# Attention and routed experts on one core: sink sums, denominators and small routing operations on GpSimd, the steps of a group in another order, the last residual added by VectorE

## The chip, the core and the metric

One core of a Trainium2 chip. The time is that of one execution on the device, in microseconds, the median of several. Engines: TensorE (PE in the profile), VectorE (DVE), ScalarE (ACT), GpSimd (POOL), and SyncE (SP), which issues most DMAs. Each engine works through its own instructions in order; between engines there are only semaphores.

## The reference

```python
x = x + attn(layernorm(x), W_qkv, W_out, s)      # x: 4 x 512 x 256
x = x + moe(layernorm(x), gating_w, w1, b1, w2, b2)

# attn: 32 query heads, 8 key/value heads, head size 64
q, k, v = split(x @ W_qkv);  q, k = rope(q), rope(k)
a = where(band mask, -inf, q k^T / 8)             # 512 x 512 for each head
w = softmax(concat([a, sink]))[..., :-1]          # one sink logit for each head
out = (w v) @ W_out

# moe: 8 experts, top 2, capacity 640 rows for each expert
gates = softmax(x @ gating_w);  weights, experts = top_k(gates, 2), normalised
position of each (token, choice) within its expert = running count
rows of each expert: relu(rows w1 + b1) w2 + b2, weighted and added to the token
```

All is float32.

## The kernel before, in words

The attention of a batch is worked off by key/value head: a group `g` is one batch and one key/value head with its four query heads, 32 groups in all, and each has 16 units `n` (head and row tile of 128 queries by 512 keys). `all_periods` (L300) walks the engines through 33 periods of 16 steps. At step `n` of period `g` it calls the engine's step function three times: `step(n, g)`, `step(n - 16, g + 1)` (preparing the next group) and `step(n + 16, g - 1)` (finishing the last one). The tables `PROJ_AT`, `ROT_AT`, `PV_AT` and so on (L283 to L294) say at which `n` of a group a piece is done, from -16 to 31. Since all engines walk through the same order, these tables are the order of each engine's queue.

PE (L1106): at every even step two score matmuls (a pair, L1120), each into one of three banks, so a pair waits for the row maximum of the first unit of the pair before. After them, by the tables: one of three projections of the next group (KV at -16, Q01 at -12, Q23 at -6, L1094), the turning of v (-8, L1101), the products of the last group with v in four pieces of 5, 3, 5 and 3 blocks (18, 20, 22, 24, L1139), and the output projection y in two halves (28, 30, L1152).

DVE (L853): for every unit the mask, scaling, row maximum and copy to SBUF in one instruction (L858), two units behind it a 32 by 32 transpose of two units of probabilities (L869). At 16 the sink logit plus row maximum for 16 units (`sink_arg`, L876), at 17 the denominator (`denom`, L886), its reciprocal and the turning of it. SP sends that through DRAM to `recip_wide` (L411, L419); at 26 and 27 DVE multiplies the four banks of P·V by it (`heads_sb`, L902).

ACT (L684): the exponential with its row sum for every unit (L691), copies of the projected chunk from PSUM one step after each projection (L673), of v (L681), the sink exponential at 16 (L703), and copies of y at 29 and 31 (L699).

POOL (L575): rotates each projected chunk (L568 to L571) once SP has copied the swapped halves of it (L374: two DMAs for KV, four for Q01 and Q23); KV at -13, Q01 at -8, Q23 at -2. After KV it splits the weights of a later group in high and low part (L539, L541). It adds y to the residual (L588) at 29 and 31. The first pair of a group waits for Q01's rotation and a second copy of k (`k_twice`), pair 8 for Q23's.

SP, for each group: swap of KV, reciprocals out and spread, swap of Q01, `k_twice`, load of weights, v out and in, for three groups the load of the next batch's normalised x, swap of Q23, and for the first eight groups zeroes for the slot rows.

Routing of batch b runs in the 96 steps that begin two periods after its last group's first step (`dve_route`, L924, and the like for other engines): statistics, root and transposes in the first 32, normalisation, logits in 32 to 47, top two, gates, weights, counting and slots in 48 to 63, and eight indirect DMAs on POOL, from 64 on, that scatter rows to expert slots (L605). Nearly all small sums were DVE's. For the last batch the same steps run alone, after all groups. Then the eight experts follow.

Of the kernel before, what the change touches and what calls it, by code (L numbers as in the profile page):

```python
# [59 lines left out]
def moe_layer(nc, x, w_qkv, w_out, sink, gate_w, w1, b1, w2, b2, rope, out):  # L60
    ctx = ExitStack()
    with ctx:
# [112 lines left out]
        s_centred = sem("s_centred")  # L175
        s_shifted = sem("s_shifted")
        s_gate_exp = sem("s_gate_exp")
# [152 lines left out]

# [19 lines left out]
        def _(sp):  # L350
# [113 lines left out]
            for g in range(GROUPS - 1):  # L464
# [52 lines left out]
        def _(pool):  # L517
# [57 lines left out]
            def pool_step(n, g, j):  # L575
# [6 lines left out]
                if n in RESIDUAL_AT:  # L582
# [7 lines left out]

            def pool_route(r, b, last):
                if r == IDS_AT:
                    if b > 0:
                        pool.wait_ge(s_scattered, b * (16 * TPB * TOPK))
                    nc.gpsimd.iota(xn2[:, :, D:D + 1].bitcast(U32), pattern=[[P, TPB], [0, 1]], base=b * L,
                                   channel_multiplier=1).then_inc(s_ids, 1)
                if r in SCATTER_AT:
                    c = SCATTER_AT[r]
                    if c == 0:
                        pool.wait_ge(s_routed, b + 1)  # L600
                        pool.wait_ge(s_zero_rows, 16 * E)
                        pool.wait_ge(s_ids, b + 1)
                    if c % TOPK == 0:
                        pool.wait_ge(s_norm2, b * TPB + c // TOPK + 1)
# [49 lines left out]
        def _(act):  # L654
# [29 lines left out]
            def act_step(n, g, j):  # L684
# [9 lines left out]
                if n in RESIDUAL_AT:  # L694
# [6 lines left out]
                if n == SINK_AT:  # L701
                    act.wait_ge(s_sink_arg, g + 1)
                    nc.scalar.activation(sink_exp[:, :], sink_arg[:, :], ACT.Exp).then_inc(s_sink_exp, 1)  # L703
# [26 lines left out]
            def act_route(r, b, last):  # L730
# [12 lines left out]
                if r == INDEX_AT:  # L743
# [64 lines left out]
        def _(dve):  # L808
# [44 lines left out]
            def dve_step(n, g, j):  # L853
# [20 lines left out]
                if n == SINK_AT:  # L874
                    dve.wait_ge(s_neg_max, g * UNITS + UNITS)
                    nc.vector.tensor_tensor(  # L876
                        sink_arg[:, :].rearrange("p (c t h) -> p c t h", c=PAIRS, h=2),
                        neg_max[j][:, :].rearrange("p (c t h) -> p c t h", c=PAIRS, h=2),
                        sink_all[:, (g % NKV) * QM:(g % NKV + 1) * QM].rearrange("p (c h) -> p c h", h=2).unsqueeze(2)
                        .broadcast_to([P, PAIRS, TPB, 2]), ALU.add).then_inc(s_sink_arg, 1)  # L880
                if n == RECIP_AT:
                    dve.wait_ge(s_probs, g * UNITS + UNITS)
                    dve.wait_ge(s_sink_exp, g + 1)
                    if later(g):
                        dve.wait_ge(s_recip_out, g * 16)
                    nc.vector.tensor_tensor(denom[:, :], sums[j][:, :], sink_exp[:, :], ALU.add).then_inc(s_denom, 1)  # L886
                    dve.wait_ge(s_denom, 2 * g + 1)

                    nc.vector.reciprocal(recip[:, 0:UNITS].rearrange("p (c h t) -> p c t h", c=PAIRS, h=2),
                                         denom[:, :].rearrange("p (c t h) -> p c t h", c=PAIRS, h=2)  # L890
                                         ).then_inc(s_denom, 1)
                    dve.wait_ge(s_denom, 2 * g + 2)
                    nc.vector.transpose(recip_t[:, :], recip[:, :]).then_inc(s_recip, 1)
                if n in HEADS_AT:
# [11 lines left out]
                    ins.then_inc(s_heads, 1)  # L906
            nc.vector.memset(recip[:, :], 0.0)
# [16 lines left out]
            def dve_route(r, b, last):  # L924
# [19 lines left out]
                if r == MEAN_PART_AT:  # L944
                    step(nc.vector.tensor_tensor(mean_part[:, :, :],
                                                 mean_var[:, 0:TPB, 0].unsqueeze(2).broadcast_to([P, TPB, E]),
                                                 gate_cols[:, :].unsqueeze(1).broadcast_to([P, TPB, E]), ALU.mult))

                if r == CENTRE_AT:
                    dve.wait_ge(s_logits, b + 1)  # L950
                    nc.vector.tensor_tensor(logits[:, :, :], PV[2][:, 0:TPB * E].rearrange("p (t e) -> p t e", e=E),
                                            mean_part[:, :, :], ALU.subtract).then_inc(s_centred, 1)
                if r == SCALE_AT:
                    dve.wait_ge(s_centred, b + 1)
                    step(nc.vector.tensor_tensor(logits[:, :, :], logits[:, :, :],
                                                 rstd[:, 0:TPB].unsqueeze(2).broadcast_to([P, TPB, E]), ALU.mult))
                if r == TOP_AT:
                    for t in range(TPB):
                        nc.vector.max(top_val[:, t, :], logits[:, t, :]).then_inc(s_top, 1)
                if r == SHIFT_AT:  # L960
                    dve.wait_ge(s_top, b * (2 * TPB) + TPB)
                    nc.vector.tensor_tensor(gates[:, :, :], logits[:, :, :],
# [356 lines left out]
```

## Time and profile before

| | |
|---|---|
| median of 3 runs | 1205.47 us (1203.82 to 1209.72) |
| profiled execution | 1205.47 us, its span 1203.7 us |
| PE busy | 1084.9 us, 90% |
| DVE busy | 936.7 us, 78% |
| POOL busy | 711.7 us, 59% |
| ACT busy | 642.7 us, 53% |

The groups of attention take the span up to about 920 us, the routing of the last batch and the way to the first expert up to 952 us, the experts the rest. A row of the timeline has the start, the duration, the engine, the line of the kernel, the operation, what it writes and reads, and how many instructions were merged in it; in brackets stand the idle time of the engine just before and who ended it.

### The profile page before, as it was taken

To read this page: it belongs to the slowest core of one execution; us is meant where nothing else is said; L and a number is where in the kernel's file an instruction comes from. 1 tells how busy PE (TensorE), PEld (TensorE's weight loads), DVE (VectorE), ACT (ScalarE), POOL (GpSimd) and SP (SyncE) were. 2 spreads that over 40 slices of the span, in tenths; PEclk is the share of its full clock that TensorE was granted. 3 is DMA by queue.
4 is the path that set the end of the run, shared out by engine and by line. 5 is a ranking of instruction groups with operands and counts; after the bars stand their busy time and mean duration, and the time that the engine had idled before them with its cause. 6 is when DMAs were issued, how large, how long until landed. Compare 5 with 4: busy or idle time off the path is not lost. (4 is left out here: it accounts for less than half of the span.)

```text
span 1203.7 us, 30733 instructions
## 1 busy us (share of the span) xinstructions
PE 1084.9 (90%) x12411; PEld 724.5 (60%) x12411; DVE 936.7 (78%) x2001; ACT 642.7 (53%) x1517; POOL 711.7 (59%) x534
## 2 busy tenths in 40 slices
PE   3589999999999999999899999989986499999996
PEld 1345555555555555555555555555545499999995
DVE  6789999889998989999898999888894144444442
ACT  1455665556755655575556657555553244555551
POOL 5566666666556776666586666567621555555552
PEclk9699999999999999999999999999997599999998
DMA  8343533333332422334333223223232414444441
GB/s 208 133 112 108 154 102 95 110 105 84 96 110 69 110 75 73 87 94 117 79 108 91 69 73 98 77 74 92 78 113 72 152 19 110 111 111 111 109 110 19
DMA packets 116286, 117.94 MB, mean 98 GB/s; under 512 B 35184, under 2 KB 103856, under 8 KB 115248
## 3 DMA queue, kind: packets, MB, share of 16 engines
q1 hardware_dynamic: 108848, 107.43, 30.9%
q0 software_dynamic: 7296, 8.55, 4.3%
q8 instruction: 98, 1.61, 0.6%
q14 instruction: 44, 0.36, 0.1%
HBM read 77.31 MB, written 24.97 MB: 85 GB/s over the span
## 5 line engine op out<-in xcount | busy, mean ns | idle before, releaser
L691 ACT ACTIVATE probs_ring<-probs_ring,neg_max 128x512 f32<-128x512 f32 x512 | 367.0, 717 | 349.0 <-DVE neg_max L858 348.7
L858 DVE CUSTOM_DVE_ANT_0 probs_ring<-bank,mask,sink_neg 128x512 f32<-128x512 f32 x512 | 365.4, 738 | 78.1 <-PE bank L1120 76.7
L869 DVE STREAM_TRANSPOSE probs_t<-probs_ring 128x1024 f32<-128x1024 f32 x256 | 317.0, 1238 | 0.0
L1120 PE MATMUL bank<-qk_st 64*128 64x512 f32 x1024 | 291.4, 646 | 17.0 <-DVE neg_max L858 15.5
L1139 PE MATMUL bank<-probs_t,v_quads 32*64 32x256 f32 x8192 | 258.3, 385 | 30.3 <-DVE probs_t L869 29.9
L1139 PEld LDWEIGHTS bank<-probs_t,v_quads 32*64 32x64 f32 x8192 | 175.5, 133 | 121.0 <-DVE probs_t L869 56.9
L568 POOL TENSOR_TENSOR chunk_sb<-chunk_sb,rope_sb 128x512 f32<-128x512 f32 (+1 forms) x96 | 123.2, 1283 | 158.6 <-DMA swap_sb<-chunk_sb 92.6
L588 POOL TENSOR_TENSOR x_sb<-x_sb,y_sb 128x512 f32<-128x512 f32 x64 | 81.6, 1275 | 179.2 <-ACT y_sb L699 179.1
L1120 PEld LDWEIGHTS bank<-qk_st 64*128 64x128 f32 x1024 | 77.4, 185 | 111.8 <-issue 66.2
L1094 PE MATMUL bank<-xcur,w_hi 128*128 128x512 f32 x384 | 132.6, 427 | 5.4 <-ACT v_next L681 3.5
L1152 PE MATMUL bank<-wo_sb,heads_sb 128*128 128x256 f32 x512 | 127.3, 392 | 0.9 <-DVE heads_sb L902 0.9
L1152 PEld LDWEIGHTS bank<-wo_sb,heads_sb 128*128 128x128 f32 x512 | 92.1, 189 | 58.3 <-issue 46.2
L571 POOL TENSOR_TENSOR qk_st<-chunk_sb,swap_sb 128x512 f32<-128x512 f32 (+1 forms) x96 | 122.5, 1276 | 7.5
L569 POOL TENSOR_TENSOR swap_sb<-swap_sb,rope_sb 128x512 f32<-128x512 f32 (+1 forms) x96 | 123.3, 1285 | 0.0
L1094 PEld LDWEIGHTS bank<-xcur,w_hi 128*128 128x128 f32 x384 | 66.0, 192 | 88.1 <-issue 49.1
L691 ACT ACTIVATION_READ_ACCUMULATOR probs_ring<-probs_ring,neg_max 128x1 f32 x512 | 95.4, 186 | 0.0
L1269 PE MATMUL bank<-w_hi,hidden_hi 128*128 128x256 f32 x320 | 91.0, 284 | 0.0
L784 ACT ACTIVATE hidden<-bank,b_sb 128x320 f32<-128x320 f32 x128 | 60.6, 525 | 56.4 <-PE bank L1256 56.4
L1269 PE MATMUL bank<-w_hi,hidden_lo 128*128 128x256 f32 x320 | 90.3, 282 | 0.0
L1269 PE MATMUL bank<-w_lo,hidden_hi 128*128 128x256 f32 x320 | 90.3, 282 | 0.0
L640 POOL TENSOR_TENSOR w_lo<-w_raw,w_hi 128x2048 fp32r<-128x2048 f32 x8 | 36.8, 4596 | 88.0 <-ACT w_hi L762 76.9
L1256 PE MATMUL bank<-slots_hi,w_hi 128*128 128x320 f32 x256 | 80.3, 314 | 1.4 <-issue 1.4
(127 smaller groups left out, 1493.3 us busy)
## 6 DMA issues: line engine op xcount, KB each, us to landing
v_quads<-v_rows SPq DMA_DIRECT2D x128, 128.0 KB, 2.6
recip_wide<-recip_rows SPq DMA_DIRECT2D x64, 256.0 KB, 4.4
w_raw<-in_L_ffn_w SPq DMA_DIRECT2D x16, 1024.0 KB, 6.6
swap_sb<-chunk_sb SPq DMA_DIRECT2D x320, 32.0 KB, 2.2
w_raw<-in_L_attn_W_qkv SPq DMA_DIRECT2D x32, 256.0 KB, 2.9
slot_rows<-x2T SPq DMA_DIRECT2D x8, 662.5 KB, 5.0
slots<-slot_rows SPq DMA_DIRECT2D x8, 662.5 KB, 4.0
w_raw<-in_L_attn_W_qkv SPq DMA_DIRECT2D x64, 64.0 KB, 2.7
```

The lines of the kernel that those rows point to most:

```text
L568: nc.gpsimd.tensor_tensor(straight, straight, rope_sb[rows, 0, :], ALU.mult).then_inc(s_pool, 1)
L569: nc.gpsimd.tensor_tensor(swapped, swapped, rope_sb[rows, 1, :], ALU.mult).then_inc(s_pool, 1)
L571: nc.gpsimd.tensor_tensor(qk_st[j][rows, PAIRS if c == KV else c - Q01, :], straight, swapped, ALU.add).then_inc(s_rot, 1)
L588: nc.gpsimd.tensor_tensor(x_sb[:, t:t + 2, :], x_sb[:, t:t + 2, :], y_sb[half][:, :, :], ALU.add).then_inc(s_residual, 1)
L691: nc.scalar.activation(probs[n % RING][:, :], probs[n % RING][:, :], ACT.Exp, bias=neg_max[j][:, n:n + 1], scale=-1.0, accum_out=sums[j][: ...
L858: nc.vector.tensor_tensor_reduce(probs[n % RING][:, :], SCORE[SCORE_OF[n // 2][n % 2]][:, :], mask[:, L - P - t * P:2 * L - P - t * P], -S ...
L869: nc.vector.transpose(probs_t[j][:, :, (h // 2) * (2 * P):(h // 2 + 1) * (2 * P)] .rearrange("p b (h q) -> p h b q", h=2)[:, :, :, t * BLK ...
L1094: ins = nc.tensor.matmul(PROJ[:, :], w[:, kc, chunk_cols(c)], xcur[g // NKV % 2][:, part, kc, :], start=(kc == 0 and m == 0), stop=(kc == ...
L1120: nc.tensor.matmul(SCORE[SCORE_OF[n // 2][hh]][:, :], qk_st[j][half, h // 2, t * P:(t + 1) * P], qk_st[j][half, PAIRS, :], start=True, sto ...
L1139: ins = nc.tensor.matmul(PV[a][p * HD:(p + 1) * HD, 0:2 * P], v_quads[j][rows, d, c * HD:(c + 1) * HD], probs_t[j][rows, blk, p * 2 * P:(p ...
L1152: ins = nc.tensor.matmul(PV[half][:, (a % 2) * D:(a % 2 + 1) * D], heads_sb[:, a, h * P:(h + 1) * P], wo_sb[:, bass.ds((g % NKV) * 2 + h, ...
L1269: ins = nc.tensor.matmul(FFN2[s][:, 0:D], a[:, c, s * P:(s + 1) * P], w[:, c, :], start=(c == 0 and m == 0), stop=(c == HC - 1 and m == 2))
```

## The change

The tables become (the others stay):

```diff
-        PROJ_AT = {-16: KV, -12: Q01, -6: Q23}
-        TURN_V_AT, V_NEXT_AT = -8, -7
-        ROT_AT = {-13: KV, -8: Q01, -2: Q23}
-        for n, blocks in [(18, 5), (20, 3), (22, 5), (24, 3)]:
-        SINK_AT, RECIP_AT = 16, 17
-        HEADS_AT = {26: 0, 27: 1}
-        Y_AT = {28: 0, 30: 1}
-        RESIDUAL_AT = {29: 0, 31: 1}
+        PROJ_AT = {-16: KV, -8: Q01, -2: Q23}
+        TURN_V_AT, V_NEXT_AT = -4, -3
+        ROT_AT = {-12: KV, -5: Q01, 2: Q23}
+        for n, blocks in [(18, 5), (20, 5), (22, 6)]:
+        SINK_AT, DENOM_AT, RECIP_AT = 16, 17, 19
+        HEADS_AT = {24: 0, 25: 1}
+        Y_AT = {26: 0, 28: 1}
+        RESIDUAL_AT = {27: 0, 29: 1}
...
-        TURN_X_AT = 16 + 12
-        X2T_AT = {16 + 13: 0, 16 + 14: 1}
+        TURN_X_AT = 16 + 14
+        X2T_AT = {16 + 15: 0, 32: 1}
-        IDS_AT = 32 + 9
-        LOGITS_AT = {32 + 12: 0, 32 + 14: 1}
-        MEAN_PART_AT, CENTRE_AT, SCALE_AT = 32 + 13, 32 + 15, 48
-        TOP_AT, SHIFT_AT, INDEX_AT, ONEHOT_AT, CHOSEN_AT = 49, 50, 51, 52, 53
-        GATE_SUM_AT, GATES_AT, TOP_SUM_AT, WEIGHTS_AT = 54, 55, 56, 58
-        COUNT_AT = 48 + 12
-        PLACE_AT, PICK_AT, SLOT_AT = 48 + 13, 48 + 14, 48 + 15
-        SCATTER_AT = {64: 0, 64 + 10: 1, 64 + 12: 2, 64 + 14: 3, 80: 4, 80 + 10: 5, 80 + 12: 6, 80 + 14: 7}
+        IDS_AT, MEAN_PART_AT = 32 + 9, 32 + 10
+        LOGITS_AT, CENTRE_AT, SCALE_AT = 32 + 14, 32 + 15, 48
+        TOP_AT, SHIFT_AT, INDEX_AT, GATE_EXP_AT, ONEHOT_AT, CHOSEN_AT = 50, 51, 51, 52, 53, 54
+        GATE_SUM_AT, GATES_AT, TOP_SUM_AT, WEIGHTS_AT = 54, 56, 57, 59
+        COUNT_AT = 48 + 14
+        PLACE_AT, PICK_AT, SLOT_AT, INDICES_AT = 48 + 15, 64, 66, 67
+        SCATTER_AT = {72: 0, 73: 1, 74: 2, 78: 3, 79: 4, 88: 5, 89: 6, 90: 7}
```

In SP's queue the swap of Q01 moves behind `k_twice` and the load of weights:

```diff
-                swap_halves(g + 1, Q01)
                 k_twice(g + 1, (g + 1) % 2)
                 if g + 3 < GROUPS:
                     load_w(g + 3, (g + 3) % 2)
+                swap_halves(g + 1, Q01)
```

The sink sum and the denominator leave DVE for POOL, with the same operands; DVE keeps the reciprocal and its turning, which wait for `s_denom`, and ACT's sink exponential waits for the denominator of the group before:

```diff
+                if n == SINK_AT:
+                    pool.wait_ge(s_neg_max, g * UNITS + UNITS)
+                    nc.gpsimd.tensor_tensor(
...
+                        .broadcast_to([P, PAIRS, TPB, 2]), ALU.add).then_inc(s_sink_arg, 1)
+                if n == DENOM_AT:
+                    pool.wait_ge(s_probs, g * UNITS + UNITS)
+                    pool.wait_ge(s_sink_exp, g + 1)
+                    if later(g):
+                        pool.wait_ge(s_recip, g)
+                    nc.gpsimd.tensor_tensor(denom[:, :], sums[j][:, :], sink_exp[:, :], ALU.add).then_inc(s_denom, 1)
```

In the routing of batches 0 to 2 eight products and sums of 32 or 64 elements and the update of `slot_base` go to POOL; for the last batch they stay on DVE. One of them stands for all:

```diff
+                if r == GATES_AT and not last:
+                    pool.wait_ge(s_gate_inv, b + 1)
+                    scale_gates(nc.gpsimd).then_inc(s_gates, 1)
+                    pool.wait_ge(s_gates, b + 1)
+                    pool.wait_ge(s_chosen, b + 1)
+                    gates_of_chosen(nc.gpsimd).then_inc(s_top_gates, 1)
```

The others are `mean_part_of`, `scale_logits`, `shift_logits`, `mark_chosen`, `weights_of`, `pick`, each at its step of the table. The two halves of the logits become one stretch of matmuls.

In the last group ACT's copies of y and POOL's residual adds are replaced by

```diff
+                if n in RESIDUAL_AT and g == GROUPS - 1:
+                    half = RESIDUAL_AT[n]
+                    t = (B - 1) * TPB + 2 * half
+                    dve.wait_ge(s_y, 2 * g + half + 1 + 1)
+                    dve.wait_ge(s_residual, 2 * g + half)
+                    nc.vector.tensor_tensor(x_sb[:, t:t + 2, :], x_sb[:, t:t + 2, :],
+                                            PV[half][:, :].rearrange("p (t d) -> p t d", t=2),
+                                            ALU.add).then_inc(s_residual, 1)
```

## Rows read from the trace of the kernel before

**Rows 1.** Page, busy time: us, share of the span, instructions.

```profile
PE 1084.9 (90%) x12411; PEld 724.5 (60%) x12411; DVE 936.7 (78%) x2001; ACT 642.7 (53%) x1517; POOL 711.7 (59%) x534
```

**Rows 2.** Timeline of ACT, sink exponentials: start us, us, engine, line, operation.

```profile
283.73 0.22 ACT L703 ACTIVATE sink_exp<-sink_arg 128x16 f32<-128x16 f32 x1
...
370.89 0.20 ACT L703 ACTIVATE sink_exp<-sink_arg 128x16 f32<-128x16 f32 x1
...
475.36 0.22 ACT L703 ACTIVATE sink_exp<-sink_arg 128x16 f32<-128x16 f32 x1
...
501.54 0.22 ACT L703 ACTIVATE sink_exp<-sink_arg 128x16 f32<-128x16 f32 x1
...
586.50 0.20 ACT L703 ACTIVATE sink_exp<-sink_arg 128x16 f32<-128x16 f32 x1
...
717.00 0.22 ACT L703 ACTIVATE sink_exp<-sink_arg 128x16 f32<-128x16 f32 x1 [0.15 <-DVE sink_arg L876]
...
802.48 0.20 ACT L703 ACTIVATE sink_exp<-sink_arg 128x16 f32<-128x16 f32 x1
```

**Rows 3.** Timeline of one plain period, 457 to 478 us; idle time before in brackets.

```profile
457.52 1.13 PE L1120 MATMUL bank<-qk_st 64*128 64x512 f32 x4
...
460.93 1.13 PE L1120 MATMUL bank<-qk_st 64*128 64x512 f32 x4
...
463.71 1.13 PE L1120 MATMUL bank<-qk_st 64*128 64x512 f32 x4
...
464.87 0.75 DVE L858 CUSTOM_DVE_ANT_0 probs_ring<-bank,mask,sink_neg 128x512 f32<-128x512 f32 x1 [0.19 <-PE bank L1120]
...
466.36 1.13 PE L1120 MATMUL bank<-qk_st 64*128 64x512 f32 x4
...
467.00 0.72 ACT L691 ACTIVATE probs_ring<-probs_ring,neg_max 128x512 f32<-128x512 f32 x1 [0.52 <-DVE neg_max L858]
...
467.72 0.57 ACT L673 ACTIVATE chunk_sb<-bank 128x512 f32<-128x512 f32 x1
...
469.48 1.13 PE L1120 MATMUL bank<-qk_st 64*128 64x512 f32 x4
...
472.46 1.13 PE L1120 MATMUL bank<-qk_st 64*128 64x512 f32 x4
...
475.92 1.23 DVE L869 STREAM_TRANSPOSE probs_t<-probs_ring 128x1024 f32<-128x1024 f32 x1
...
477.21 2.42 PE L1139 MATMUL bank<-probs_t,v_quads 32*64 32x256 f32 x80 [0.97 <-DVE probs_t L869]
```

**Rows 4.** Tile sink_arg (min/median/max ns), then POOL groups (busy us, mean ns).

```profile
L876 DVE TENSOR_TENSOR sink_arg<-neg_max,sink_all x32: 131/1031/1198, 73.8 to 904.9; 128x16 f32<-128x16 f32 x32
...
L595 POOL IOTA xn<- 128x4 uint32 x4 | 0.6, 140 | 0.0
```

**Rows 5.** Timeline and landings of the Q01 swap; last, a Q23 swap's landings.

```profile
457.46 2.46 SPq L374 DMA_DIRECT2D swap_sb<-chunk_sb  x4
...
462.79 1.28 POOL L568 TENSOR_TENSOR chunk_sb<-chunk_sb,rope_sb 128x512 f32<-128x512 f32 x1 [2.38 <-DMA swap_sb<-chunk_sb]
...
465.39 1.29 POOL L571 TENSOR_TENSOR qk_st<-chunk_sb,swap_sb 128x512 f32<-128x512 f32 x1
...
DMA to landing us min/median/max: 2.5/3.0/3.3
...
DMA to landing us min/median/max: 2.0/2.0/2.2
```

**Rows 6.** Timeline, first period's pairs and the last residual add.

```profile
60.36 1.13 PE L1120 MATMUL bank<-qk_st 64*128 64x512 f32 x4 [1.27 <-DVE neg_max L858]
...
71.59 1.13 PE L1120 MATMUL bank<-qk_st 64*128 64x512 f32 x4 [1.44 <-DVE neg_max L858]
...
921.58 1.26 POOL L588 TENSOR_TENSOR x_sb<-x_sb,y_sb 128x512 f32<-128x512 f32 x1 [0.77 <-ACT y_sb L699]
```

More of the change, by code:

```diff
@@ new lines, in shift_logits, with mark_chosen, scale_gates @@
+        def shift_logits(eng):
+            return eng.tensor_tensor(gates[:, :, :], logits[:, :, :],
+                                     top_val[:, :, 0].unsqueeze(2).broadcast_to([P, TPB, E]), ALU.subtract)
+        def mark_chosen(eng):
+            return eng.tensor_tensor(chosen[:, :, :], onehot[:, :, 0, :].bitcast(F32),
+                                     onehot[:, :, 1, :].bitcast(F32), ALU.add)
+        def scale_gates(eng):
+            return eng.tensor_tensor(gates[:, :, :], gates[:, :, :],
+                                     gate_sum[:, :].unsqueeze(2).broadcast_to([P, TPB, E]), ALU.mult)
@@ L580, in pool_step @@
                         split(g + 1, 1 - j, (g + 1) // 2)
-                if n in RESIDUAL_AT:
+                if n in RESIDUAL_AT and g < GROUPS - 1:
                     half = RESIDUAL_AT[n]
@@ L596, in pool_route @@
                                    channel_multiplier=1).then_inc(s_ids, 1)
+                if r == MEAN_PART_AT and not last:
+                    pool.wait_ge(s_rstd, b + 1)
+                    mean_part_of(nc.gpsimd).then_inc(s_mean_part, 1)
+                if r == SCALE_AT and not last:
+                    pool.wait_ge(s_centred, b + 1)
+                    scale_logits(nc.gpsimd).then_inc(s_scaled, 1)
+                if r == SHIFT_AT and not last:
+                    pool.wait_ge(s_top, b * (2 * TPB) + TPB)
+                    shift_logits(nc.gpsimd).then_inc(s_shifted, 1)
+                if r == CHOSEN_AT and not last:
+                    pool.wait_ge(s_onehot, b + 1)
+                    mark_chosen(nc.gpsimd).then_inc(s_chosen, 1)
+                if r == GATES_AT and not last:
[4 more added lines that the diff above has]
+                    gates_of_chosen(nc.gpsimd).then_inc(s_top_gates, 1)
+                if r == WEIGHTS_AT and not last:
+                    pool.wait_ge(s_top_inv, b + 1)
+                    weights_of(nc.gpsimd).then_inc(s_weights, 1)
+                if r == PICK_AT and not last:
+                    pool.wait_ge(s_place, b + 1)
+                    pick(nc.gpsimd).then_inc(s_picked, 1)
+                    nc.gpsimd.tensor_tensor(slot_base[:, :], slot_base[:, :], batch_total[:, :],
+                                            ALU.add).then_inc(s_slot_base, 1)
                 if r in SCATTER_AT:
@@ L702, in act_step @@
                     act.wait_ge(s_sink_arg, g + 1)
+                    if later(g):
+                        act.wait_ge(s_denom, g)
                     nc.scalar.activation(sink_exp[:, :], sink_arg[:, :], ACT.Exp).then_inc(s_sink_exp, 1)
@@ L961, in dve_route @@
                     dve.wait_ge(s_top, b * (2 * TPB) + TPB)
-                    nc.vector.tensor_tensor(gates[:, :, :], logits[:, :, :],
-                                            top_val[:, :, 0].unsqueeze(2).broadcast_to([P, TPB, E]),
-                                            ALU.subtract).then_inc(s_shifted, 1)
+                    if last:
+                        shift_logits(nc.vector).then_inc(s_shifted, 1)
                 if r == INDEX_AT:
@@ L976, in dve_route @@
                                             ALU.mult, ALU.add)
-                    dve.wait_ge(s_onehot, b + 1)
-                    step(nc.vector.tensor_tensor(chosen[:, :, :], onehot[:, :, 0, :].bitcast(F32),
-                                                 onehot[:, :, 1, :].bitcast(F32), ALU.add))
+                    if last:
+                        dve.wait_ge(s_onehot, b + 1)
+                        mark_chosen(nc.vector).then_inc(s_chosen, 1)
                 if r == GATE_SUM_AT:
@@ L1020, in dve_route @@
                                                    ALU.mult, ALU.add).then_inc(s_routed, 1)
-                    if not last:
-                        step(nc.vector.tensor_tensor(slot_base[:, :], slot_base[:, :], batch_total[:, :], ALU.add))
             dve.wait_ge(s_gate_cols, 1)
```

118 lines of the change are left out of this document (70 added, 48 removed).

## The prediction

> **What bounds the kernel now.** The page first: over the span PE is busy 90%, DVE 78%, POOL 59% [rows 1]. A share of 90% says that PE nearly bounds, not what its idle time waits for. So I read one period (16 steps, 8 pairs of score matmuls) from the timeline. The sink exponentials of ACT, one in each period, give its length: 501.54 − 475.36 = 26.18 us in a plain period, and 87.16, 84.96 and 85.48 us for the three periods together in which the steps of routing of a batch lie (370.89 − 283.73, 586.50 − 501.54, 802.48 − 717.00) against 78.5 for three plain ones [rows 2]. Routing costs 8.6 + 6.4 + 6.9 = 22 us.
>
> In the plain period the start times of the score pairs [rows 3] give the length of each PE slot, a pair (1.06 us to the next matmul) with what follows it: pair 10 to 12 (a projection) 466.36 − 463.71 = 2.65; 6 to 8 (five blocks of P·V) 460.93 − 457.52 = 3.41; 14 to 0 (half of y) 2.98; 12 to 14 (the other half) 3.12, of which about 0.14 is a wait for a row maximum; 8 to 10 (turning v, three blocks) 2.78. A K/V projection is as long as the others. The one large wait is at the first P·V block: 0.97 us for a DVE transpose [rows 3]. Followed back, DVE works without a pause from 464.87 (it had waited 0.19 for pair 10) to the end of that transpose at 475.92 + 1.23 = 477.15, and in that stretch lies the sink sum, 1.03 us in the median [rows 3, 4]. So the loop that sets the period is PE from P·V to pair 10, then DVE to the transpose: neither engine alone. PE without any wait would need about 25 us.
>
> **The change, part by part.**
>
> *Sink sum and denominator to POOL.* The sink sum takes 131 ns at the least and 1031 in the median on DVE [rows 4]; 0.95 of the period's DVE chain goes. The denominator stands behind the transpose, off that chain; its removal and the three steps by which the reciprocal comes later only give DVE slack. On POOL no add of 16 elements is in the trace. From below I take the iota of 4 elements, 140 ns [rows 4]; from above an add of 512 elements, 1.26 [rows 4, 6]. I take 0.2, by the iota. POOL then holds, from the period's start, two residual adds (2.5), sink sum (to 2.7), denominator after ACT's exponential (to 3.3); the swapped Q23 chunk lands at about 4.5, so even 1.26 each is hidden in a plain period. Queued behind a late denominator are the rotations of Q23 and K/V; Q23 is wanted at 13.4.
>
> Why the DVE form takes up to 1.2 us: its minimum is 0.13 and the rest is about one POOL add long, as if it waited for POOL. The Trainium skill (SBUF — State Buffer, Who interferes with whom) says that a DVE instruction with two SBUF inputs and a GpSimd one that reads SBUF exclude each other for the whole instruction; by that rule the trace agrees (131 against 1031 ns). The skill (Perfetto Trace Analysis, Optimizing Scalar/DVE Operations) warns that moving work between those two might therefore not help; by it the removal would still take the 0.9 of waiting off DVE, and POOL could at worst wait for a short DVE add.
>
> *The order of a group.* New PE slots, from the same rows: 0: K/V projection 2.65; 2: P·V of five 3.41; 4: five 3.41; 6: six 3.41 + 0.47 = 3.88; 8: Q01 projection 2.65; 10: y 2.98; 12: turning v (2.78 − 1.06 − 1.48 for three blocks = 0.24) and y 3.22; 14: Q23 2.65. The transpose for the first P·V ends at 1.16 + 2 × 0.67 + 1.24 + 0.06 = 3.8 after pair 0, PE is there at 3.71: wait 0.1. Pair 0 to pair 8 is 13.45. DVE has 16 reductions of at most 0.75, 8 transposes of 1.23, four head products (two take about 0.7 of the 2.13 below) and under 1 for the reciprocal: 12.0 + 9.8 + 1.4 + 1.0 = 24.2 at most, less than PE's 25, and is no bound.
>
> But Q01 is projected at pair 8 in place of 4, and its rotation must be done before pair 0 of the next group. That chain, from pair 8: to the DVE reduction 1.16 (463.71 to 464.87); reduction, two head products, reduction, to ACT's exponential 2.13 (to 467.00); to the chunk copy 0.72 (467.72), its 0.57 and 0.03 to the first of four swap DMAs; the last of these is issued 1.88 later and lands after 2.0 to 2.2 in quiet queues, so 4.05 to the rotation; the rotation 3.87 (462.79 to 465.39 + 1.27); 0.08 to PE [rows 3, 5]. Sum 12.61. PE's own path over these slots is 2.65 + 2.98 + 3.22 + 2.65 = 11.50 and 0.14 of a wait as now: 11.64. So the old wait of 1.0 goes and a new one of 1.0 comes, for the rotation at pair 0. Period: 13.45 + 12.61 = 26.06 against 26.18, −0.1. Of the 31 periods between the first sink exponential and the last, nine hold routing; 22 plain ones give −2.6 (−0.12 each).
>
> In the trace the swap of Q01 takes longer, 457.46 to 462.79 = 5.33, its landings 2.5 to 3.3 [rows 5]. There it runs behind the spread of the reciprocals. In the new order the spread is issued at about 8.6 after pair 0 and the swap at 18, so I take the quiet value; the loaded one is a rival. In SP's queue the swap is now behind the copy of k (after the K/V rotation, near 12.2) and the loads of w (to 15), which are through before 18. The reciprocals land at about 13.7; the head products ask at 15.3.
>
> *Routing.* First of the three periods: statistics and roots stay where they were, with their two ACT table loads; v's copy now comes behind these, so Q23 and the eight transposes at pair 14 end late: 27.6 (now 27.5). Second: PE has 1.9 us of logits on its path, 13.45 + 11.64 + 1.9 = 27.0. Third: the eight small VectorE products are on POOL, in front of which stand rotations. The shift of the logits waits for the rotation of Q23, which load of a batch delays to about 11; ACT's queue and five exponentials wait with it, within their slack. The chosen gates follow the K/V rotation and the split of w, near 18.8; DVE asks at 18.45 and then has 0.8 of sums of its own: pair 12 comes 1.25 late, and the counting takes PE 1.3. 13.45 + 11.64 + 1.25 + 1.3 = 27.65; in the last batch, with no load ahead, 26.4. Sums 82.25, 82.25, 81.05 against 87.16, 84.96, 85.48: −12.1 in all [rows 2]. The scatters, now in bunches of two and three, fall in POOL's gap before the Q01 rotation, or delay a sink sum by 2.6 with DVE slack behind it: nothing taken, at most 0.5 per batch.
>
> *Start and end.* The first period has no P·V over which PE could be busy; pair 8 stood at 60.36 and the next pair 0 at 71.59 [rows 6]. The new chain from there is 12.61 − 0.66 (no head products) + 0.45 (DVE behind) = 12.4: +1.2. The last scoring period has P·V in bigger pieces and is DVE's: +0.4. At the end the second residual add, now 1.26 on POOL from 921.58 [rows 6], is on DVE from about 920.9 and some 0.7 long (the head product of 256 elements is 0.35); the four statistics move behind it, but the root's table load is no longer behind the last x copy: −1.2.
>
> **The sum.** −2.6 − 12.1 + 1.2 + 0.4 − 1.2 = −14.3 on a span of 1203.7. The profiled run took 1205.47, 1.8 outside the span, and is also the median of the three shown. Forecast 1191.2 us.
>
> **Rivals.**
>
> A, *the Q01 swap stays slow* (5.33 instead of 4.05). For it: that is its value in every period now, with POOL waiting; against: its company in the queues is gone. Price: the plain period is 27.3, 22 × 1.28 = +28 on the forecast, 1219, slower than before. It decides from 0.65 us above my value, where it eats the 14.3.
>
> B, *the chain is shorter than PE's path*, 11.64 or less, since chunk copy or landing come earlier than in any row. Then a plain period is 25.1: 22 × 0.97 = 21 less, 1170. For it: the landings' minimum is 1.9 to 2.0; against: it wants 1 us off a chain of which 7.7 is measured computation.
>
> C, *POOL as an in-order queue gives routing's gain back*: small operations near 1.27 rather than 0.2, or behind a rotation that comes later. Chosen gates are three in a row, +3 us per batch, and shift, gates and weights each hold DVE or ACT once; 4 us per batch gives 12: 1203, no change. For it: rotations of 3.9 stand ahead of each; against: iota at 140 ns.
>
> **How the numbers follow.** Forecast case 0.54 (0.50 of it faster by over 0.5%, which is about what a measurement can tell here, 0.04 within). A 0.18 (0.15 slower, 0.03 same). B 0.10, faster. C 0.18 (0.02 faster, 0.14 same, 0.02 slower). So faster 0.62, same 0.21, slower 0.17. The forecast's own range is ±0.3 us in a plain period, 1184 to 1199; towards B and half-way to A the eight-in-ten range is 1175 to 1211.
>
> **What would show it.** Right: the wait of PE for the transpose at the first P·V falls from 0.97 to about 0.1, and PE waits some 1.0 before pair 0 for POOL's rotated chunk; plain periods of 26.06; sink sum at 0.2 on POOL; the third routing period at 26.4 to 27.7. Wrong: a Q01 swap over 4.7 us, DVE waiting for POOL's denominator, or a plain period under 25.6, which would say that the chain to pair 0 is not the bound.

## The result and the profile after

The changed kernel takes 1308.29 us in the median of 4 runs (1302.46 to 1311.54), the kernel before 1205.93 beside it (1203.82 to 1209.72): ratio 1.084, 95% interval 1.079 to 1.089. The forecast was 1191.2 with a range up to 1211. Faster was forecast; what came is 102 us slower.

The page's busy line of the changed kernel, then three of its groups (busy us, mean ns, then idle time before and what ended it):

```profile
PE 1124.2 (86%) x12411; PEld 746.7 (57%) x12411; DVE 894.4 (68%) x1912; ACT 635.2 (49%) x1515; POOL 725.3 (56%) x623
...
L609 POOL TENSOR_TENSOR chunk_sb<-chunk_sb,rope_sb 128x512 f32<-128x512 f32 (+1 forms) x96 | 122.1, 1272 | 328.4 <-DMA swap_sb<-chunk_sb 318.4
...
L1176 PE MATMUL bank<-xcur,w_hi 128*128 128x512 f32 x384 | 148.2, 471 | 75.9 <-ACT chunk_sb L755 71.7
...
L781 ACT ACTIVATE y_sb<-bank 128x512 f32<-128x512 f32 x62 | 36.2, 585 | 108.2 <-POOL x_sb L629 108.2
```

Against [rows 1], DVE has 42 us less work, as the edits intend, and no engine is nearer to its limit. Two waits are new, and each occurs once in 29 of the 32 groups: ACT's copy of y waits for POOL's residual add, 108.2 us in all, and PE's first projection matmul waits for ACT's copy of a chunk, 71.7. The list of waits gives counts and the longest of them:

```profile
ACT y_sb L781 <- POOL x_sb L629: 108.2, 29, 4.8
...
PE bank L1176 <- ACT chunk_sb L755: 71.7, 29, 2.8
```

The timeline of the changed kernel around one period's end shows how the two hang together:

```profile
540.82 2.46 SPq L415 DMA_DIRECT2D swap_sb<-chunk_sb  x4
...
543.39 0.57 ACT L781 ACTIVATE y_sb<-bank 128x512 f32<-128x512 f32 x1
...
544.78 1.28 POOL L609 TENSOR_TENSOR chunk_sb<-chunk_sb,rope_sb 128x512 f32<-128x512 f32 x1 [5.76 <-DMA swap_sb<-chunk_sb]
...
547.38 1.28 POOL L612 TENSOR_TENSOR qk_st<-chunk_sb,swap_sb 128x512 f32<-128x512 f32 x1
...
548.61 1.26 POOL L629 TENSOR_TENSOR x_sb<-x_sb,y_sb 128x512 f32<-128x512 f32 x1
...
549.97 0.60 ACT L781 ACTIVATE y_sb<-bank 128x512 f32<-128x512 f32 x1 [3.75 <-POOL x_sb L629]
...
550.47 0.71 ACT L773 ACTIVATE probs_ring<-probs_ring,neg_max 128x512 f32<-128x512 f32 x1
...
551.87 0.58 ACT L755 ACTIVATE chunk_sb<-bank 128x512 f32<-128x512 f32 x1
...
552.00 1.25 DVE L953 STREAM_TRANSPOSE probs_t<-probs_ring 128x1024 f32<-128x1024 f32 x1 [0.70 <-ACT probs_ring L773]
...
552.60 0.94 PE L1176 MATMUL bank<-xcur,w_hi 128*128 128x512 f32 x2 [2.76 <-ACT chunk_sb L755]
```

Half 0 of y is copied at 543.39, in time. Its add (548.61) stands in POOL's queue behind the rotation of Q01 (both fall on step 11 of a period: −5 + 16 and 27 − 16). The rotation waits for the swap's transfers until 544.78. ACT's copy of half 1 asks for `s_residual` at `2 * g + half`: it waits for the add of half 0 of its own group, although the two halves have their own buffers. So it starts at 549.97, and behind it in ACT's queue stand the last two exponentials and, at 551.87, the copy of the Q23 chunk out of the projection's bank; for that bank PE's K/V projection waits 2.76 us, and DVE's transpose 0.70 for the exponentials. In the kernel before, add 0 (step 29) stood clear of both rotations, and ACT waited for an add only once in the whole run, for 1.4 us.

The windows of three periods of the changed kernel, between sink exponentials (length, busy time and count of each engine, granted clock, DMA share, GB/s):

```profile
463.40:493.60 30.20, 26.58 (x327) 14.74 (x326) 22.27 (x47) 15.10 (x42) 16.79 (x15) 0.91 0.27 70
493.60:524.50 30.90, 27.30 (x328) 15.29 (x327) 22.22 (x47) 15.04 (x41) 16.79 (x15) 0.92 0.26 67
524.50:553.10 28.60, 25.01 (x328) 14.41 (x327) 22.27 (x47) 15.10 (x42) 16.81 (x15) 1.00 0.27 74
```

The third runs at a granted clock of 1.00 (2.4 GHz throughout) and is 2.7 us longer than a plain period without the wait (25.90, below): the wait itself. The other two show 0.91 and 0.92. Each of the three begins just behind a wait of PE of 2.76 us (to 462.95, 493.11 and 524.03). Behind the second, the windows from 493 to 498 us show a granted clock of 0.50, which is the lower level, 1.2 GHz, at which PE works on without a pause; behind the third, the window from 523 to 526 us shows 1.00. The same matmuls take PE 26.58 and 27.30 us in the two longer periods instead of 25.01. So the same wait costs 2.7 us in one period and 4.3 to 5.0 in another. Over the whole run the mean clock is 0.931; before it was 0.969.

### The profile page after: what moved, and what is told of

It reads as the page before. It is cut to its first block, busy times and chain, and to the rows that moved or that the text cites. A ratio compares the mean times of both kernels' runs of the same rounds, so it can differ in the third digit from the quotient of the medians.

```text
span 1306.1 us, 30776 instructions
## 1 busy us (share of the span) xinstructions
PE 1124.2 (86%) x12411; PEld 746.7 (57%) x12411; DVE 894.4 (68%) x1912; ACT 635.2 (49%) x1515; POOL 725.3 (56%) x623
## 3 DMA queue, kind: packets, MB, share of 16 engines
q1 hardware_dynamic: 108848, 107.43, 28.8%
## 4 chain that ended last, share of the span: by engine, by line
PE 53%; POOL 13%; DVE 8%; DMA 8%; issue 7%; ACT 6%; SPq 4%; POOLq 0%; ACTq 0%; DVEq 0%
PE bank L1221 17%; PE bank L1202 12%; PE bank L1349 9%; PE bank L1336 8%; PE bank L1176 6%; DMA swap_sb<-chunk_sb 5%; SPq L415 4%; ACT probs_ring L773 3%; POOL qk_st L612 3%; POOL chunk_sb L609 3%; POOL swap_sb L610 3%; POOL x_sb L629 3%; DVE probs_ring L942 3%; ACT chunk_sb L755 2%; DVE heads_sb L975 2%
## 5 line engine op out<-in xcount | busy, mean ns | idle before, releaser
L1202 PE MATMUL bank<-qk_st 64*128 64x512 f32 x1024 | 310.4, 685 | 31.9 <-POOL qk_st L612 19.8
L1221 PE MATMUL bank<-probs_t,v_quads 32*64 32x256 f32 x8192 | 251.8, 385 | 6.0 <-DVE probs_t L953 5.3
L1221 PEld LDWEIGHTS bank<-probs_t,v_quads 32*64 32x64 f32 x8192 | 179.8, 134 | 119.8 <-issue 86.0
L1176 PE MATMUL bank<-xcur,w_hi 128*128 128x512 f32 x384 | 148.2, 471 | 75.9 <-ACT chunk_sb L755 71.7
L1176 PEld LDWEIGHTS bank<-xcur,w_hi 128*128 128x128 f32 x384 | 73.8, 213 | 161.7 <-issue 122.0
L1202 PEld LDWEIGHTS bank<-qk_st 64*128 64x128 f32 x1024 | 82.8, 198 | 136.8 <-issue 62.9
L629 POOL TENSOR_TENSOR x_sb<-x_sb,y_sb 128x512 f32<-128x512 f32 x62 | 78.7, 1269 | 38.7 <-ACT y_sb L781 38.5
L781 ACT ACTIVATE y_sb<-bank 128x512 f32<-128x512 f32 x62 | 36.2, 585 | 108.2 <-POOL x_sb L629 108.2
L1176 PE MATMUL bank<-xcur,w_lo 128*128 128x512 f32 x192 | 87.4, 455 | 0.0
```

Of the source, the lines that this page charges most:

```text
L629: nc.gpsimd.tensor_tensor(x_sb[:, t:t + 2, :], x_sb[:, t:t + 2, :], y_sb[half][:, :, :], ALU.add).then_inc(s_residual, 1)
L1176: ins = nc.tensor.matmul(PROJ[:, :], w[:, kc, chunk_cols(c)], xcur[g // NKV % 2][:, part, kc, :], start=(kc == 0 and m == 0), stop=(kc == ...
L1202: nc.tensor.matmul(SCORE[SCORE_OF[n // 2][hh]][:, :], qk_st[j][half, h // 2, t * P:(t + 1) * P], qk_st[j][half, PAIRS, :], start=True, sto ...
L1221: ins = nc.tensor.matmul(PV[a][p * HD:(p + 1) * HD, 0:2 * P], v_quads[j][rows, d, c * HD:(c + 1) * HD], probs_t[j][rows, blk, p * 2 * P:(p ...
```

## Experiments

Nine kernels ran; those with one run each have no interval. A sink interval is the time from one sink exponential of ACT to the next, and stands for the length of a period. Theory W: the loss is ACT's wait for the add of its own group, which the new place of the Q01 rotation made late.

**One wait freed (e1).** The changed kernel, with

```diff
-                        act.wait_ge(s_residual, 2 * g + half)
+                        act.wait_ge(s_residual, 2 * g)
```

> The changed kernel, but ACT's copy of the second half of y waits for 2g residual adds (all adds of the groups before, the last readers of its buffer) and no longer for the first add of its own group. Theory W: in the changed kernel that copy waits for an add that stands in POOL's queue behind the rotation of Q01, which waits for the swap DMAs, and ACT's two last exponentials and the Q23 chunk copy stand behind the copy; with the wait gone the plain period falls from 30.2 to about 26.1 us and the kernel to about 1191 us (1183 to 1200). Rival R1 (the late projection of Q01 and its chain to pair 0 are by themselves the loss): the period stays above 29 us, the kernel above 1280. Rival R2 (POOL's new small operations hold POOL's queue): same as R1, above 1280.

Measured: 1203.8 us (1200.49 to 1205.86), ratio to before 0.998 (0.996 to 1.000), clock 0.967. W is shown: one number in one wait is worth 104 us. The plain period came as expected; the time is 4 us above the range given, and where it sits is told in the next section. Two windows of its plain periods and the rows at one period's end:

```profile
451.30:477.20 25.90, 25.01 (x328) 14.42 (x330) 22.15 (x47) 15.16 (x39) 16.84 (x15) 1.00 0.30 81
477.20:503.10 25.90, 25.00 (x328) 14.42 (x330) 22.16 (x47) 15.16 (x39) 16.84 (x15) 1.00 0.32 81
```

```profile
465.90 0.58 ACT L755 ACTIVATE chunk_sb<-bank 128x512 f32<-128x512 f32 x1
466.50 2.46 SPq L415 DMA_DIRECT2D swap_sb<-chunk_sb  x4
...
470.46 1.28 POOL L609 TENSOR_TENSOR chunk_sb<-chunk_sb,rope_sb 128x512 f32<-128x512 f32 x1 [6.60 <-DMA swap_sb<-chunk_sb]
...
473.06 1.28 POOL L612 TENSOR_TENSOR qk_st<-chunk_sb,swap_sb 128x512 f32<-128x512 f32 x1
...
474.40 0.30 PEld L1202 LDWEIGHTS bank<-qk_st 64*128 64x128 f32 x4 [1.21 <-POOL qk_st L612]
```

PE works 25.01 us and stands still for 0.9, before pair 0, for the rotated chunk.

**The add first (e2).** The wait kept, POOL's add 0 at step 26, ahead of the rotation.

```diff
         RESIDUAL_AT = {27: 0, 29: 1}
+        POOL_RESIDUAL_AT = {26: 0, 29: 1}
...
-                if n in RESIDUAL_AT and g < GROUPS - 1:
-                    half = RESIDUAL_AT[n]
+                if n in POOL_RESIDUAL_AT and g < GROUPS - 1:
+                    half = POOL_RESIDUAL_AT[n]
```

> The changed kernel with the copy's wait as it was, but POOL's first residual add one step earlier, at step 26, so that it stands ahead of the rotation of Q01 and not behind it. Theory W: the copy's wait ends before it is reached, ACT is free; the rotation of Q01 may start up to 0.6 us later, since the add (1.27 us) ends after the swap has landed: plain period 26.1 to 26.7, kernel 1191 to 1210 us. R1 and R2: no gain, above 1280.

In one run: 1224.17 us, clock 0.964, 14 above the range given. The second way of lifting the wait gives 84 us back. Its plain periods are 26.4 to 28.8 us, not the 25.9 of the first way. The add now stands between the swap and the rotation, and PE waits 38.0 us in all (26 times) for the rotated chunk, against 20.0 (21 times) in e1: 18 of the 20 us between the two kernels.

**The order alone (e4).** The changed kernel with sink sum and denominator back on DVE at steps 16 and 17.

```diff
-        SINK_AT, DENOM_AT, RECIP_AT = 16, 17, 19
+        SINK_AT, RECIP_AT = 16, 17
```

> The changed kernel with the sink sum and the denominator back on DVE at steps 16 and 17, all else as changed. Theory W and R1: the order is the loss, the kernel stays at 1300 to 1320 us and ACT's copy of y still waits 3.7 us for POOL. R2: the loss goes, 1190 to 1215 us.

In one run: 1307.9 us, and ACT's copy of y waits 107.4 us for the add in 29 groups, 3.7 each. The loss is there without the sinks' move: it belongs to the order.

**The move alone (e3).** The kernel before, with sink sum and denominator on POOL and the reciprocal at step 19.

```diff
-        SINK_AT, RECIP_AT = 16, 17
+        SINK_AT, DENOM_AT, RECIP_AT = 16, 17, 19
```

> The kernel before, in its old order, with only the sink sum and the denominator on POOL and the reciprocal two steps later. The loop of the period before ran over PE and a stretch of DVE that held the sink sum (about 0.95 us). If my reading of that loop holds: PE's wait for the transpose falls from 0.97 to about 0.1, the plain period from 26.18 to about 25.2, the kernel to 1173 to 1185 us. Rival R2 (the small operations on POOL cost as much as they save, by waits of ACT or of POOL's queue): 1200 us or more. Rival R3 (the two engines exclude each other, so that POOL now waits where DVE did): sink sum on POOL near 1 us, gain under 10 us.

Measured: 1207.45 us (1204.57 to 1214.64), ratio 1.000 (0.997 to 1.003): not the 1173 to 1185 expected, but what R2 said; R3 falls, since the sum takes 0.22 us on POOL. Its plain periods are of two kinds, as its sink exponentials show:

```profile
158.63 0.22 ACT L720 ACTIVATE sink_exp<-sink_arg 128x16 f32<-128x16 f32 x1 [2.88 <-POOL sink_arg L594]
...
183.84 0.21 ACT L720 ACTIVATE sink_exp<-sink_arg 128x16 f32<-128x16 f32 x1 [2.86 <-POOL sink_arg L594]
...
209.07 0.22 ACT L720 ACTIVATE sink_exp<-sink_arg 128x16 f32<-128x16 f32 x1 [2.88 <-POOL sink_arg L594]
...
236.12 0.21 POOL L594 TENSOR_TENSOR sink_arg<-neg_max,sink_all 128x16 f32<-128x16 f32 x1
236.37 0.21 ACT L720 ACTIVATE sink_exp<-sink_arg 128x16 f32<-128x16 f32 x1 [4.96 <-POOL sink_arg L594]
...
237.32 1.25 DVE L886 STREAM_TRANSPOSE probs_t<-probs_ring 128x1024 f32<-128x1024 f32 x1 [3.44 <-ACT probs_ring L706]
```

25.2 us (183.84 − 158.63, 209.07 − 183.84), and 27.3 (236.37 − 209.07). In the old order the sink sum stands behind the Q23 rotation and an add in POOL's queue. ACT waits for it with the next exponentials behind; where that wait is 2.9 us it is slack, where it is 5.0 the period is 2 longer. Of the 18 intervals outside routing and before the last, seven are 25.1 to 25.2 us, all with a wait of 2.8 to 2.9; the other eleven are 25.7 to 28.2, nine of them with a wait of 3.5 to 5.8. Why the sink sum comes later in some periods than in others is not shown. If what VectorE gained is lost in that wait, a later consumer must bring it back. The next kernel tests that.

**The exponential of the sinks later (e5).** The kernel e3, with ACT's exponential behind exponential 3, and the denominator ahead of the K/V rotation on POOL.

```diff
-        SINK_AT, DENOM_AT, RECIP_AT = 16, 17, 19
+        SINK_AT, SINK_EXP_AT, DENOM_AT, RECIP_AT = 16, 19, 19, 20
...
-                if n == SINK_AT:
+                if n == SINK_EXP_AT:
                     act.wait_ge(s_sink_arg, g + 1)
```

> The order of before, with the two sink operations on GpSimd as in e3_offload_only, but ScalarE's exponential of the sinks waits until behind exponential 3 of the next group (step 19, not 16), the denominator follows it on GpSimd ahead of the K/V rotation, and the reciprocal stands at step 20. Theory Q (e3's gain was lost because sink_arg stands behind the Q23 rotation and residual add 1 in GpSimd's queue, and ScalarE with exponentials 0, 1 behind its wait for it): sink_arg is as late as in e3 (about 5 us into ScalarE's wait there), but ScalarE then meets it done; its wait on sink_arg goes from 102 us in all to under 15, and all 14 plain periods come out at 25.1 to 25.4. Routing periods follow before's order and stay near e3's best ones (26.6). Total 1207.5 - about 25 = 1178 to 1188 us. Rival R (e3's long periods come from something else that the POOL wait only shadows, such as the Q01 swap transfers behind the reciprocal's round trip on SP's queue): periods of 26.6 to 29.5 remain and the time stays above 1198. A second rival: the denominator now holds the K/V rotation on GpSimd and the reciprocal's round trip holds SP's swap of Q01, which brings waits of GpSimd on swap_sb and 27 us periods, total 1200 to 1225.

Measured: 1190.88 us (1187.36 to 1192.13) against 1210.19 in the same runs, ratio 0.983 (0.980 to 0.985). ACT waits 19.0 us for the sink sum instead of 102.4. Of the sink intervals, the first eight together take 203.3 us, 25.4 each (kernel before: 208.7), and four plain ones in the middle 101.2 (104.4). Single ones are uneven, 22.5 to 29.8, and not all 25.1 to 25.4 as expected. With the wait gone the gain of the move is there, which is what theory Q says; the denominator and the reciprocal moved with it and were not tried apart; the time is 3 us above the range given, since the routing periods kept their length (112.9, 111.4 and 109.3 us for three times four periods, against 113.4, 110.6 and 112.9).

**Only the denominator on POOL (e7).** The kernel before, its sink sum still on DVE at step 16.

```diff
+                if n == DENOM_AT:
+                    pool.wait_ge(s_probs, g * UNITS + UNITS)
+                    pool.wait_ge(s_sink_exp, g + 1)
...
+                    nc.gpsimd.tensor_tensor(denom[:, :], sums[j][:, :], sink_exp[:, :], ALU.add).then_inc(s_denom, 1)
```

> The order of before with only the denominator on GpSimd (step 17) and the reciprocal at step 19; sink_arg stays on VectorE at step 16. Theory Q: ScalarE no longer waits for GpSimd's queue, so there are no periods of 27 to 29.5 us; VectorE keeps 0.22 us more than in e3, so plain periods are 25.3 to 25.7 instead of 25.1 and all alike; total 1186 to 1195 us. Rival R: the long periods remain, total 1200 to 1210.

Measured: 1209.19 us (1203.28 to 1215.22), ratio 0.998 (0.996 to 1.001): no gain. This expectation was wrong, by its size of the sink sum: it took 0.22 us for what stays on DVE, where the tile's rows of this run (minimum, median, maximum in ns) say

```profile
L886 DVE TENSOR_TENSOR sink_arg<-neg_max,sink_all x32: 134/1030/1433, 75.0 to 909.3; 128x16 f32<-128x16 f32 x32
```

as [rows 4] had said before. On POOL the same sum takes 217 ns in the median (e3). Plain periods are 26.17 as in the kernel before: the whole microsecond that the move brings is the sink sum, and the denominator brings nothing, which is what the prediction had said of both.

**Two transfers in the changed order (e6).** The kernel e1, with the first expert's weights loaded behind the reciprocals of group 30, and two scatters moved off the period's end.

```diff
-        SCATTER_AT = {72: 0, 73: 1, 74: 2, 78: 3, 79: 4, 88: 5, 89: 6, 90: 7}
+        SCATTER_AT = {72: 0, 73: 1, 74: 2, 75: 3, 76: 4, 88: 5, 89: 6, 90: 7}
...
-            sp.dma_start(w1_raw[:, :, :], w1[0].rearrange("(c p) n -> p c n", p=P)).then_inc(s_w1_in, 16)
...
             recip_spread(GROUPS - 2)
+            sp.dma_start(w1_raw[:, :, :], w1[0].rearrange("(c p) n -> p c n", p=P)).then_inc(s_w1_in, 16)
```

> e1_early_copy (the changed kernel with ScalarE's copy of y freed from the add of its own group) with two more edits: SP issues the first expert's weight loads behind the reciprocals of group 30 instead of ahead of them, and the scatters of steps 78 and 79 stand at 75 and 76, ahead of the Q23 rotation. If the loads were what held the last spread of reciprocals (issued 7 us behind its rows' transfer in e1), the last scoring period falls from 27.7 to 23 to 24 us; if the two scatters held sink_arg, the 13th, 21st and 29th sink intervals fall from 28.6 to 26.7 (and the following ones of 24.6 rise to about 25.9, as those made up for it): net 3 times 0.7 to 1.9. Expected total 1203.8 - 4.5 - 2 to 5 = 1194 to 1198 us. Rivals: another transfer or wait holds them, and the intervals stay; then 1203 to 1205.

Measured: 1196.94 us (1195.44 to 1201.79), ratio 0.989 (0.986 to 0.991). The last scoring period, the one between the sink exponentials of groups 30 and 31, falls from 27.7 to 22.7. The rows of e1 show why:

```profile
877.31 1.07 SPq L525 DMA_DIRECT2D w_raw<-in_L_ffn_w  x1
878.43 0.48 SPq L526 DMA_DIRECT2D w_raw<-in_L_ffn_w  x1
880.48 0.34 SPq L452 DMA_DIRECT2D recip_rows<-recip_t  x1
887.45 1.32 SPq L460 DMA_DIRECT2D recip_wide<-recip_rows  x2
...
893.56 0.76 DVE L975 TENSOR_TENSOR heads_sb<-bank,recip_wide 128x256 f32<-128x256 f32 x2 [3.35 <-issue]
```

16 KB of reciprocals, issued 2 us behind two loads of 1 MB, take 7 us to land. With the loads behind them the spread is issued 1.4 us after (878.85, 880.29). In the kernel before the loads stood ahead of the reciprocals too, but 7.0 us ahead, and the spread followed 2.3 us after the rows:

```profile
878.38 0.47 SPq L485 DMA_DIRECT2D w_raw<-in_L_ffn_w  x1
...
885.34 0.34 SPq L411 DMA_DIRECT2D recip_rows<-recip_t  x1
887.69 1.32 SPq L419 DMA_DIRECT2D recip_wide<-recip_rows  x2
```

The scatters' half fell: the three periods named go from 28.6, 29.6 and 28.6 us to 28.4, 29.4 and 28.4, because the moved scatters now hold POOL's second add, and with it the sink sum, for nearly the same time:

```profile
395.50 1.00 POOL L686 DMA_INDIRECT slot_rows<-xn,scatter_idx  x1 [0.16 <-POOL x_sb L628]
...
396.80 0.98 POOL L686 DMA_INDIRECT slot_rows<-xn,scatter_idx  x1 [0.30 <-issue]
...
399.29 0.22 ACT L786 ACTIVATE sink_exp<-sink_arg 128x16 f32<-128x16 f32 x1 [2.35 <-POOL sink_arg L633]
```

That the time still lies in the expected range is in part luck: the profiled runs differ by 8.5 us (1204.1 and 1195.6), of which 5.0 are in the last scoring period; 2.7 lie ahead of the first sink exponential and 1.9 behind the last, where no row ties them to either edit.

**The zeroing transfers (e8).** The kernel e6, with `zero_rows` behind `recip_spread` on SP.

```diff
                     recip_spread(g - 1)
+                if 0 < g <= E:
+                    zero_rows(g - 1)
...
-                if g < E:
-                    zero_rows(g)
```

> e6_late_weights_early_scatters with one more edit: the transfer that zeroes 662 KB of the experts' slots in each of eight groups is issued behind the spread of the reciprocals, instead of behind the Q23 swap and so just ahead of the next K/V swap and of the reciprocals' own rows. In e6 the sink intervals 3, 5 and 6 are 27.4 to 28.2 us where plain ones are 25.9, and VectorE's heads wait up to 1.65 us for the spread there. If that transfer holds the reciprocals, these intervals fall to 26.0 to 26.3 and the first eight together from 212.7 to 208 to 209.5: total 1192 to 1194 us. Rival: it now holds the Q01 swap instead, whose rotation releases the next group's scores: then all of the first eight rise by 1 to 3 us and the total is 1200 or more.

Measured: 1198.26 us (1194.53 to 1202.67), ratio 0.992 (0.989 to 0.995), no different from e6 (0.989, 0.986 to 0.991). The first eight intervals take 211.2 us instead of 212.7 and one of them is still 28.1. The theory gets at most 1.5 of its 4 us; what holds these periods stays open.

**Two routing operations (e9).** The kernel e5, and of the routing only the weights' product and the running slot base, a sum, on POOL.

```diff
+                if r == WEIGHTS_AT + 1 and not last:
+                    pool.wait_ge(s_top_inv, b + 1)
+                    nc.gpsimd.tensor_tensor(xn2[:, :, D + 1:ROW], gates[:, :, :],
...
+                if r == SLOT_AT and not last:
+                    pool.wait_ge(s_place, b + 1)
+                    nc.gpsimd.tensor_tensor(slot_base[:, :], slot_base[:, :], batch_total[:, :],
```

> e5_sink_exp_late (order of before, sinks on GpSimd, exponential late) with only two routing operations of three batches on GpSimd: the weights' product (1.12 us on VectorE in e5) and the running slot base (1.24 us), each at a place where GpSimd waits for a transfer. If VectorE bounds the routing periods, as its rows of e5 say, each batch gives back 2.3 us less what its waits take: 112.9 + 111.4 + 109.3 us for three times four periods fall by 4 to 7 us in all, total 1184 to 1188. Rival: the routing periods are held elsewhere (Q01 rotation, ScalarE), then the time stays at 1190 to 1192; or GpSimd's own wait for VectorE's reciprocal at step 59 delays the v rotation and adds: 1193 to 1198.

Measured: 1179.32 us (1175.25 to 1183.88) against 1206.82 in the same runs, ratio 0.977 (0.974 to 0.980): the fastest kernel of this study, in the old order. Its three times four routing periods take 108.9, 108.6 and 107.3 us, 8.8 less in all than without the two edits. That is more than the 4 to 7 expected, and the time is 5 us below the range given; the profiled run (span 1173.5) is some 4 us faster than its kernel's median, so the surplus is not to be relied on. By the ratios, e9 is 0.6% faster than e5, about 7 us. The expectation had the weights' product at 1.12 us on VectorE. In e5 that is so in one batch; in the two others, and in all three of the kernel before, it takes 0.19. The slot base takes 1.24 in all three batches. So the two operations held VectorE for 5.2 us in e5, less than the time that was won; the two were not tried apart, and what the rest of the gain comes from is open. The slot base, its tile in this kernel and in the kernel before (count, ns, first and last start):

```profile
L627 POOL TENSOR_TENSOR slot_base<-slot_base,batch_total x3: 202/208/210, 359.4 to 776.8; 128x8 f32<-128x8 f32 x3
```

```profile
L1022 DVE TENSOR_TENSOR slot_base<-slot_base,batch_total x3: 1235/1237/1237, 368.1 to 799.7; 128x8 f32<-128x8 f32 x3
```

## Why the prediction was wrong

**The step that failed is "The order of a group".** It followed the Q01 chain from projection to pair 0 of the next group, through the chunk copy, the swap and the rotation, and it named the queue that Q01's swap is moved past (SP's). It did not follow the queue that the rotation was moved into. On POOL the rotation now stands in front of residual add 0, and for that add ACT's second copy of y waits: 3.7 us in each of 29 groups, with PE's next projection held 2.5 us behind it (2.8 at the most) and the granted clock falling after some of these waits. The cost stood in two lines of the code, `RESIDUAL_AT` against `ROT_AT`, and `act.wait_ge(s_residual, 2 * g + half)`. With the step's own numbers it could have been priced: the rotation ends 12.5 us after pair 8, the add 1.3 later, and the copy of half 1 is asked for near pair 14. No rival held this case. C had POOL's order as its mechanism, but only for routing's small operations; A and B were about the chain's length. Freeing this one wait gives back 104 us.

The other steps, read in the run without that wait (e1, span 1204.1, forecast 1189.4):

- *Plain period*: forecast 26.06, measured 25.90; PE's wait for the transpose gone and one of 0.8 for the rotated chunk before pair 0 (1.2 at its weight load), forecast 1.0; the swap to the rotation 470.46 − 466.50 = 3.96, forecast 4.05. So rivals A and B both fell. This is the mechanism of the forecast, right as far as it went, and its gain was only ever 0.1 to 0.3 us a period. Two slips in the sums are too small to matter: the last row of the rotation is 1.29 long, not 1.27 [rows 5], and the third batch's parts give 81.0, not 81.05.
- *Sink sum and denominator*: right. 217 ns against 0.2 on POOL, 1.07 us off the plain period in the best periods of the move alone (26.18 to 25.11), and nothing from the denominator. What was not seen is that the same move in the old order makes ACT wait.
- *Routing*: forecast 108.3, 108.3 and 107.1 us for three times four periods (the step's sums and a plain one), measured 109.1, 111.4 and 108.9. The excess of 5.7 us sits in the periods with scatters at their end (28.6, 29.6 and 28.6 us, each followed by one of 24.6 to 24.8), to which the step had given "at most 0.5 per batch". The step had foreseen a sink sum 2.6 late "with DVE slack behind it"; the engine that waits for the sum is ACT, 2.55 us in each batch, with the next exponentials behind it (first row below). A long period and the short one behind it take 1.3 to 2.6 us more than two plain ones of 25.90.
- *The first eight periods*: 212.2 against 8 × 26.06 = 208.5; open, as told above.
- *Last scoring period*: forecast +0.4, measured +4.9, from the weight loads ahead of the reciprocals. The loads are issued when the last projection is done, and the change moved that projection (Q23, −6 to −2). The reciprocals hardly moved: their rows are issued 3.9 us behind the sink exponential of group 30 (880.48 − 876.63), before 3.1 (885.34 − 882.23). So the loads went from 7.0 to 2.1 us ahead of them, and the prediction did not look at that queue.
- *Start*: forecast 76.2 for the first sink exponential, measured 79.5 in this run, 76.9 in the changed kernel and 76.9 to 79.2 in four more of the same order. Runs of one order differ by 2.6 us there, so the +1.2 can't be told.
- *End*: forecast −1.2; residual adds on DVE take 0.69 each (second row), and the stretch from the last head products to the end of the root is 8.3 us against 9.8, as forecast. But from the last sink exponential to the end it is 299.8 us here and 298.7 before. Six runs of the changed order give 297.9 to 300.0, so over the whole end the −1.2 can't be told.

```profile
400.85 0.22 ACT L787 ACTIVATE sink_exp<-sink_arg 128x16 f32<-128x16 f32 x1 [2.55 <-POOL sink_arg L634]
...
921.18 0.69 DVE L985 TENSOR_TENSOR x_sb<-x_sb,bank 128x512 f32<-128x512 f32 x1 [1.04 <-PE bank L1234]
```

Start (+3.3), the first eight periods (+3.7), routing (+5.7), the last three periods (+3.3) and the end (+2.3), less 3.8 for the plain periods between the batches, make up the 14.7 us by which this run's span exceeds the forecast.

The chance of 0.17 for slower rested on the swap's speed and on POOL's queue in routing, neither of which happened. The sum of −14.3 us proved 12.6 us too low a time with the wait freed (1203.8 against 1191.2), and 5.7 with the weight loads behind the reciprocals as well (e6, 1196.9, beside which the kernel before took 1210.2 and not 1205.5).

## What to carry to other kernels

When a step is moved in an in-order queue, list the instructions that now stand behind it on its engine and, for each, every wait on its semaphore on the other engines: the change's cost was not in the moved chain but in an add queued behind it. A wait that is stricter than the data needs (half 1 waiting for half 0 of its own group) can cost nothing until the order changes, as here; loosen it first. Before work is moved to a half-idle engine, look at what stands ahead of it in that engine's queue at the moment its result is wanted, and put the consumer later rather than the work earlier.

## What the runs showed of the hardware

A wait of PE can cost more than its length, when the granted clock falls behind it: in the changed kernel a wait of 2.76 us went with a period of 28.6 us at clock 1.00 and with periods of 30.2 and 30.9 at 0.91 and 0.92, of which 1.6 and 2.3 us are longer matmuls.

A small VectorE sum with both inputs in SBUF that starts while GpSimd is in a tensor instruction ends, in these traces, with that instruction. Rows of the kernel before:

```profile
474.01 1.29 POOL L569 TENSOR_TENSOR swap_sb<-swap_sb,rope_sb 128x512 f32<-128x512 f32 x1
...
474.30 1.03 DVE L876 TENSOR_TENSOR sink_arg<-neg_max,sink_all 128x16 f32<-128x16 f32 x1
...
904.85 0.13 DVE L876 TENSOR_TENSOR sink_arg<-neg_max,sink_all 128x16 f32<-128x16 f32 x1
```

Of the 32 sink sums there, 29 start inside such an instruction, and each of them ends 0.02 to 0.04 us behind its end; the other three take 0.13 to 0.17 us. The denominator does the same (0.82 us in the median), but four that start during a scatter of GpSimd (an indirect DMA, L605) take 0.12 to 0.13. The Trainium skill (SBUF — State Buffer, Who interferes with whom) says that a VectorE instruction with two SBUF inputs and a GpSimd instruction that reads SBUF exclude each other, and these rows agree. On GpSimd the same sums take 0.19 to 0.25 us in the kernels that have them there. The kernel with four small operations moved there (sink sum, denominator, weights, slot base) and one consumer moved later is 2.3% faster (e9).
